# The first layer's attention taken by batch: four 32-row score tiles side by side, sums by a ones tile, division at the heads, mask addend on GpSimd

## The chip, the cores and the metric

The kernel runs on one core of a Trainium2 chip. Five engines work at once on their own instruction streams: TensorE (matrix products, weight loads beside them), VectorE, ScalarE, GpSimd and SyncE (which issues the transfers). They share the on-chip memory SBUF; TensorE writes into PSUM, eight banks of 128 partitions by 512 float32, and wait for one another on semaphores. The metric is the device time of one execution in microseconds (us), the median of several runs.

## The reference, cut to what matters

Four cross-attention layers run one after the other on x (16 batches of 128 tokens, 256 features) with a context of the same size. The change lies in the first, in float32:

```python
def attention(q, k, v, mask):            # 16 heads of 16 features
    scores = jnp.einsum('bhqd,bhkd->bhqk', q, k) / jnp.sqrt(jnp.float32(HD))
    scores = scores * mask - 10000.0 * (1.0 - mask)
    probs = jax.nn.softmax(scores, axis=-1)
    return jnp.einsum('bhqk,bhkd->bhqd', probs, v)
# layer 0: x += o(attention(ln1 x, ln1 x, mask 1)); x += co(attention(ln2 x, context, mask 2));
#          x += w2(gelu(w1(ln3 x)))      # 256 -> 1024 -> 256
```

Both masks are applied in full, whatever they hold.

## The kernel before

The function `layer0` (line 136) takes the batches in eight pairs (NB = 2). The attention of a pair is cut into units of four heads of one batch: a score tile of 128 queries by 4 x 128 keys fills one PSUM bank. There are U = 8 units of self attention and 8 of cross attention a pair, 4 units a batch.

All engines run the same eleven bodies of 16 steps (`bodies`, line 260): three written out, a loop over j = 3 to 7, three written out. In body g the cross units of pair g - 2 take steps 0 to 7 and the self units of pair g steps 8 to 15 (`unit`, line 268). Beside the units stands a table of linear parts (`BESIDE`, line 250), with the step and the offset of the pair: T0, T1, T2 are the transposes of the three layer norms, q, k, v and cq, ck, cv the projections, o and co the output projections, f0 to f3 the hidden parts and y0, y1 the outputs of the feed-forward. Bodies 0 and 1 have self attention alone, body 2 both attentions, bodies 3 to 7 everything, bodies 8 and 9 cross attention and feed-forward, body 10 feed-forward alone.

Each engine executes its stream in the order in which the code writes it out, so an instruction that waits holds back all behind it. A unit u goes this way:

- GpSimd, two steps ahead: `mask_keys` (line 393) copies the keys four times, each copy with all rows but those of one head set to zero (km). A product over 128 rows then gives four heads' scores at once.
- TensorE: `scores` (line 508), one product of 128 x 128 by 128 x 512. The profile shows a float32 product as two records.
- VectorE, `softmax_step` (line 737), all in step u: multiply by the mask out of PSUM into ring_e (line 748), then the reciprocal of the unit before (753), add the addend -10000 (1 - mask) (756), negated maxima (758).
- ScalarE, step u + 1: `exponentials` (614), four activations of 128 x 128, each with an accumulator for the sum of its rows.
- GpSimd, step u + 1: `norm` (406) multiplies the unit by the reciprocals (409).
- TensorE, step u + 3: `turn` (517), four transposes into the turn bank; ScalarE, step u + 4: `copy_turned` (622) into ring_t; TensorE, step u + 5: `times_v` (525), four products into column tiles of 32, at once with each other; ScalarE: `copy_heads` (627) after each second unit.

In a step TensorE does scores, linear part, `times_v`, `turn` (line 540); ScalarE exponentials, `copy_turned`, the affine or hidden part of the linear one, the tanh of the step before (`gate`), the heads (634); VectorE `softmax_step`, the reading of the linear part, the gate of the step before (`gated`), then at fixed steps statistics and normalisation of the layer norms (761). GpSimd takes the inverse deviations (`inverse_std`) and the biases of the residual (`add_bias`). The linear parts have four PSUM banks in three groups (line 216); scores have two, the turn bank and the heads' bank one each.

SyncE loads the pairs' inputs, context and masks one body ahead (line 349). After this layer a barrier follows, then the other three layers.

Of the kernel before, what the change touches and what calls it, by code (L numbers as in the profile page):

```python
# [14 lines left out]
ALU = mybir.AluOpType  # L15
# [3 lines left out]
P = 128  # L19
# [116 lines left out]
def layer0(nc, v):  # L136
# [8 lines left out]
    RE, RT, RK = 4, 2, 4  # L145

    L_E, L_T, L_P, L_V, LEAD_K = 1, 3, 4, 5, 2
    PAIR_ROWS = 2 * HD0
    with ExitStack() as ctx:  # L150
# [28 lines left out]
        qT = [sb(n, [P, 2, TOK]) for n in ("qT", "cqT")]  # L179
# [5 lines left out]
        km = sb("km", [P, RK, BANK])  # L185
        ring_e = sb("ring_e", [P, RE, BANK])
        ring_t = sb("ring_t", [P, RT, BANK])
# [3 lines left out]
        z_sum = sb("z_sum", [P, RE, QUAD])  # L191
        z_inv = sb("z_inv", [P, RE, QUAD])
# [11 lines left out]
        bq_scaled = sb("bq_scaled", [P, 4])  # L204

        def row(name):
            return rows[:, ROWS[name]:ROWS[name] + D]

        score_bank = [psum[:, j, :] for j in range(2)]
        turn_bank = psum[:, 2, :]  # L210
        pv_bank = psum[:, 3, :]

        entry = Banks(ctx, nc, "entry", ["T0", "q", "k", "v"], [psum[:, 4, :]])
        middle = Banks(ctx, nc, "middle", ["o", "T1", "ck", "cq", "cv"], [psum[:, 5, :]])
        post = Banks(ctx, nc, "post", ["co", "T2", "f0", "f1", "f2", "f3", "y0", "y1"],
                     [psum[:, 6 + j, :] for j in range(2)])
        for banks in (entry, middle, post):  # L220
            events += banks.full_ev + banks.out_ev
# [12 lines left out]
        (keys_masked, scores_done, scores_mul, scores_add, max_done, exp_done, z_inv_done, probs_done, turned,  # L234
         probsT_done, pv_done) = (event(n, STEPS, credit=2) for n in (
             "keys_masked", "scores_done", "scores_mul", "scores_add", "max_done", "exp_done", "z_inv_done",
             "probs_done", "turned", "probsT_done", "pv_done"))
        heads_out = event("heads_out", U, credit=2)
# [5 lines left out]
        dve_consts = sem("dve_consts")  # L244
        vm_zeroed = sem("vm_zeroed")
        ident_step = sem("ident_step")

        BESIDE = {0: [("T2", -3)], 1: [("f0", -3)], 2: [("T0", 0), ("f1", -3)], 3: [("q", 0)], 4: [("k", 0)],  # L250
                  5: [("f2", -3)], 6: [("o", -1)], 7: [("f3", -3)], 8: [("v", 0)], 9: [("y0", -3)],
                  10: [("T1", -1)], 11: [("y1", -3)], 12: [("ck", -1)], 13: [("co", -2)], 14: [("cq", -1)],
                  15: [("cv", -1)]}
        BODIES = R0 + 3

        LIKE = 5
# [1411 lines left out]
```

## Time and profile before

| | us |
|---|---|
| median of 3 runs | 1520.36 (1518.43 to 1522.3) |
| profiled execution | 1517.32 |
| its span, first to last instruction | 1515.6 |
| TensorE busy | 1330.7 (88%) |
| VectorE busy | 1003.3 (66%) |
| ScalarE busy | 888.4 (59%) |
| GpSimd busy | 649.5 (43%) |
| mean granted TensorE clock | 0.965 |

The rows write PE for TensorE, PEld for its weight loads, DVE for VectorE, ACT for ScalarE and POOL for GpSimd. Busy time is the union of an engine's instructions. A group of instructions is told by line, engine, operation and tiles written and read; behind the bar come the busy time, the mean of one in ns, and the idle time of its engine just before it with what ended that. TensorE's records overlap: the start of the next is a better measure of what a group costs than its own length.

### The profile page before, as it was taken

To read this page: it belongs to the slowest core of one execution; us is meant where nothing else is said; L and a number is where in the kernel's file an instruction comes from. 1 tells how busy PE (TensorE), PEld (TensorE's weight loads), DVE (VectorE), ACT (ScalarE), POOL (GpSimd) and SP (SyncE) were. 2 spreads that over 40 slices of the span, in tenths; PEclk is the share of its full clock that TensorE was granted. 3 is DMA by queue.
4 is the path that set the end of the run, shared out by engine and by line. 5 is a ranking of instruction groups with operands and counts; after the bars stand their busy time and mean duration, and the time that the engine had idled before them with its cause. 6 is when DMAs were issued, how large, how long until landed. Compare 5 with 4: busy or idle time off the path is not lost. (4 is left out here: it accounts for less than half of the span.)

```text
span 1515.6 us, 29849 instructions
## 1 busy us (share of the span) xinstructions
PE 1330.7 (88%) x9586; PEld 999.7 (66%) x9586; DVE 1003.3 (66%) x2031; ACT 888.4 (59%) x3038; POOL 649.5 (43%) x615
## 2 busy tenths in 40 slices
PE   4678898898989776589999999999999999996897
PEld 2444565565656454478888888888888888884464
DVE  3477777777777844376666666676676667664354
ACT  2476767677776734365656656555565555553443
POOL 3487676766666632023334333333333333342000
PEclk9899999999999998789999999999999999998899
DMA  4030000000000000010000000000000000000110
GB/s 158 1 140 18 5 15 3 14 10 7 10 7 3 11 0 1 28 43 2 8 1 9 0 0 7 0 7 0 0 7 0 7 0 0 2 1 1 51 42 28
DMA packets 18509, 24.54 MB, mean 16 GB/s; under 512 B 1360, under 2 KB 16912, under 8 KB 18064
## 3 DMA queue, kind: packets, MB, share of 16 engines
q1 hardware_dynamic: 18448, 23.77, 4.8%
q8 instruction: 33, 0.54, 0.2%
q14 instruction: 28, 0.23, 0.1%
HBM read 21.67 MB, written 2.10 MB: 16 GB/s over the span
## 5 line engine op out<-in xcount | busy, mean ns | idle before, releaser
L953 POOL TENSOR_TENSOR prob<-prob,l_z_inv 128x512 f32<-128x512 f32 x256 | 261.2, 1042 | 457.2 <-DVE l_z_inv L1194 457.2
L1113 ACT ACTIVATE prob<-psum,l_neg_max 128x256 f32<-128x256 f32 x512 | 236.0, 473 | 240.5 <-DVE l_neg_max L1188 240.5
L618 ACT ACTIVATE ring_e<-ring_e,neg_max 128x128 f32<-128x128 f32 x512 | 199.4, 395 | 98.8 <-DVE neg_max L758 98.3
L409 POOL TENSOR_TENSOR ring_e<-ring_e,z_inv 128x512 f32<-128x512 f32 x128 | 174.2, 1361 | 139.5 <-DVE z_inv L753 139.5
L1188 DVE TENSOR_REDUCE l_neg_max<-psum 128x2 f32<-128x512 f32 x256 | 163.9, 682 | 10.6 <-PE psum L1007 10.6
L1035 PE MATMUL psum<-pT,vs 128*64 128x256 f32 x1024 | 138.8, 391 | 6.7 <-DVE aTl L1204 6.7
L1019 PEld LDWEIGHTS psum<-ident,prob 128*128 128x128 f32 x1024 | 109.8, 141 | 49.0 <-issue 45.4
L1019 PE MATMUL psum<-ident,prob 128*128 128x128 f32 x1024 | 139.9, 280 | 0.0
L521 PE MATMUL psum<-ident,ring_e 128*128 128x128 f32 x512 | 85.7, 292 | 50.7 <-ACT ring_t L625 49.7
L1199 DVE COPY pT<-psum 128x512 f32<-128x512 f32 x128 | 88.1, 689 | 51.0 <-PE psum L1019 51.0
L521 PEld LDWEIGHTS psum<-ident,ring_e 128*128 128x128 f32 x512 | 55.8, 144 | 81.5 <-issue 77.3
L1113 ACT ACTIVATION_READ_ACCUMULATOR prob<-psum,l_neg_max 128x1 f32 x512 | 103.7, 203 | 0.0
L1204 DVE TENSOR_TENSOR aTl<-psum,aTh 128x256 fp32r<-128x256 f32 x128 | 54.4, 425 | 74.2 <-ACT aTh L1128 74.2
L618 ACT ACTIVATION_READ_ACCUMULATOR ring_e<-ring_e,neg_max 128x1 f32 x512 | 98.1, 192 | 0.0
L1035 PEld LDWEIGHTS psum<-pT,vs 128*64 128x64 f32 x1024 | 63.2, 136 | 43.0 <-issue 5.9
L758 DVE TENSOR_REDUCE neg_max<-ring_e 128x4 f32<-128x512 f32 x128 | 87.8, 686 | 4.4
L1007 PE MATMUL psum<-kh,qh 64*128 64x256 f32 x512 | 85.8, 331 | 4.2 <-ACT prob L1113 4.2
L625 ACT COPY ring_t<-psum 128x512 f32<-128x512 f32 x128 | 73.0, 570 | 19.7 <-PE psum L521 19.5
L989 PE MATMUL psum<-zuh,wzh 128*128 128x256 f32 x256 | 74.4, 291 | 11.2 <-DVE zul L1230 11.2
L471 PE MATMUL psum<-w,hid 128*128 128x256 f32 x256 | 65.5, 415 | 19.5 <-DVE hid L710 19.5
L399 POOL TENSOR_TENSOR km<-kT,head_rows 128x512 f32<-128x512 f32 x64 | 71.2, 1116 | 23.1 <-issue 13.9
L399 POOL TENSOR_TENSOR km<-ckT,head_rows 128x512 f32<-128x512 f32 x64 | 78.4, 1226 | 0.0
(196 smaller groups left out, 3510.3 us busy)
## 6 DMA issues: line engine op xcount, KB each, us to landing
wz_raw<-wz_in SPq DMA_DIRECT2D x2, 1536.0 KB, 10.4
x_in<-x SPq DMA_DIRECT2D x8, 256.0 KB, 2.7
cT<-ctxT SPq DMA_DIRECT2D x8, 256.0 KB, 2.7
w<-w_in SPq DMA_DIRECT2D x2, 1024.0 KB, 11.5
l_ub<-ctx_in SPq DMA_DIRECT2D x8, 256.0 KB, 2.8
cg<-ctx_in SPq DMA_DIRECT2D x4, 512.0 KB, 3.5
out<-fin SPq DMA_DIRECT2D x4, 512.0 KB, 2.8
wi_raw<-wi_in SPq DMA_DIRECT2D x1, 1536.0 KB, 15.2
```

Of the source, the lines that this page charges most:

```text
L399: pool.tensor_tensor(km[:, n % RK, :].rearrange("p (h k) -> p h k", h=QUAD), kT[a][:, half, b * P:(b + 1) * P].unsqueeze(1).broadcast_to([ ...
L409: pool.tensor_tensor(p, p, z_inv[:, n % RE, :].unsqueeze(2).broadcast_to([P, QUAD, P]), ALU.mult)\
L521: last = nc.tensor.transpose(turn_bank[:, h * P:(h + 1) * P], ring_e[:, n % RE, h * P:(h + 1) * P], ident[:, :])
L618: last = nc.scalar.activation(e, e, ACT.Exp, bias=neg_max[:, n % RE, h:h + 1], accum_out=z_sum[:, n % RE, h:h + 1])
L758: nc.vector.tensor_reduce(neg_max[:, n % RE, :], e, AX.X, ALU.max, negate=True)\
L953: pool.tensor_tensor(e, e, z_inv[:, t % RE, h, :].unsqueeze(2).broadcast_to([P, 2, D]), ALU.mult)\
L1007: last = mm(score_bank[h][:, qt * D:(qt + 1) * D], q[qp][rows, pair % 2, qt, b, :], k[kp][rows, pair % 2, :, b, :], start=(qp, kp) == (0, ...
L1019: last = nc.tensor.transpose(turn_bank[h][:, kt * D + qt * P:kt * D + (qt + 1) * P], prob[:, t % RE, h, qt * D + kt * P:qt * D + (kt + 1) ...
L1035: last = mm(pv_bank[h * HD1:(h + 1) * HD1, :], vs[:, pair // 2 % 2, b, kt, at:at + HD1], pT[:, h, kt * D:(kt + 1) * D], start=kt == 0, sto ...
L1113: last = nc.scalar.activation(prob[:, t % RE, h, qt * D:(qt + 1) * D], score_bank[h][:, qt * D:(qt + 1) * D], ACT.Exp, bias=neg_max[:, t % ...
L1188: nc.vector.tensor_reduce(neg_max[:, t % RE, h, :], score_bank[h].rearrange("p (t c) -> p t c", t=2), AX.X, ALU.max, negate=True).then_inc ...
L1199: nc.vector.tensor_copy(pT[:, 1, :], turn_bank[1]).then_inc(copied[1].sem, 1)
```

## The change

Lines of the change that the text speaks of; names as above.

- The queries, not the keys, are masked: `affine` for q and cq writes two copies of the transposed queries, one with the odd and one with the even heads' rows set to zero (scale and bias by `parity`), four activations in place of two. `mask_keys` and km go.
- `scores` runs once a batch, a step ahead of its first unit, at steps 3, 7, 11 and 15: 16 products with 32 rows of contraction, each on its own four rows-of-32 tile and, by tile, in its own PSUM bank (four score banks). Unit j of the batch is row tile j.
- VectorE multiplies the first two units of a batch in the first step and the other two in the second. GpSimd adds the addend (`add_mask`). The maxima follow on VectorE in the next step (L_M = 1), at its head.
- Exponentials have no accumulator, and nothing is multiplied between them and the transposes, which are in step u + 2, behind the linear part; `copy_turned` is in step u + 2 as well.
- `times_v` runs once a batch, at steps 2, 6, 10 and 14: 16 products as before, then 8 of 256 columns with a tile of ones as weights, which put the sum of each head's exponentials into the other half of the bank, on that head's rows.
- VectorE's `divide`, one step later (3, 7, 11, 15), takes the reciprocal of the sums (128 x 256, out of PSUM) and multiplies the heads by it into oT. `copy_heads` and the reciprocals of 128 x 4 go.
- The linear parts share two banks in turn. The table is written anew: cv at step 0 of the next body, f1 ahead of T0 in step 2, ck at 9, y0 at 11, co at 12, cq at 13, y1 at 15.
- Rings of eight instead of four for ring_e and of two for ring_t.

```diff
-    RE, RT, RK = 4, 2, 4
-    L_E, L_T, L_P, L_V, LEAD_K = 1, 3, 4, 5, 2
+    RE = 8
+    L_M, L_E, L_T, L_P, LEAD_S, L_V, L_N = 1, 1, 2, 2, 1, 6, 7
...
+        BESIDE = {0: [("T2", -3), ("cv", -2)], 1: [("f0", -3)], 2: [("f1", -3), ("T0", 0)], 3: [("q", 0)],
+                  4: [("k", 0)], 5: [("f2", -3)], 6: [("o", -1)], 7: [("f3", -3)], 8: [("v", 0)], 9: [("ck", -1)],
+                  10: [("T1", -1)], 11: [("y0", -3)], 12: [("co", -2)], 13: [("cq", -1)], 15: [("y1", -3)]}
...
+            def add_mask(a, i, u, ri, n):
+                e = ring_e[:, n % RE, :].rearrange("p (h k) -> p h k", h=QUAD)
+                add = (cross_add[:, u // QUAD, :] if a else self_add[:, :]).unsqueeze(1).broadcast_to([P, QUAD, P])
...
+                pool.wait_ge(*scores_mul.at(ri, n))
+                pool.tensor_tensor(e, e, add, ALU.add).then_inc(scores_add.sem, 1)
...
             def scores(a, i, u, ri, n):
...
+                for h in range(QUAD):
+                    half, t = divmod(h, 2)
+                    for j in range(QUAD):
+                        rows = slice(j * PAIR_ROWS, (j + 1) * PAIR_ROWS)
+                        last = nc.tensor.matmul(score_bank[j][:, h * P:(h + 1) * P],
+                                                qT[a][rows, t, half, b * P:(b + 1) * P],
+                                                kT[a][rows, half, b * P:(b + 1) * P], start=True, stop=True)
...
             def times_v(a, i, u, ri, n):
...
+                for half in range(2):
+                    for t in range(2):
+                        for j in range(QUAD):
+                            at, h = (2 * j + t) * PAIR_ROWS, 2 * half + t
+                            nc.tensor.matmul(pv_bank[j * PAIR_ROWS:(j + 1) * PAIR_ROWS, half * P:(half + 1) * P],
+                                             vm[a][:, b, half, at:at + PAIR_ROWS],
+                                             ring_t[:, (n + j) % RE, h * P:(h + 1) * P], start=t == 0, stop=t == 1)
+                for t in range(2):
+                    for j in range(QUAD):
+                        last = nc.tensor.matmul(pv_bank[j * PAIR_ROWS:(j + 1) * PAIR_ROWS, 2 * P:4 * P], ones[:, t, :],
+                                                ring_t[:, (n + j) % RE, :].rearrange(
+                                                    "p (c t q) -> p c t q", c=2, t=2)[:, :, t, :],
+                                                start=t == 0, stop=t == 1)
...
-                    last = nc.scalar.activation(e, e, ACT.Exp, bias=neg_max[:, n % RE, h:h + 1],
-                                                accum_out=z_sum[:, n % RE, h:h + 1])
+                    last = nc.scalar.activation(e, e, ACT.Exp, bias=neg_max[:, n % RE, h:h + 1])
...
+            def divide(a, i, u, ri, n):
...
+                dve.wait_ge(*pv_done.at(ri, n // QUAD))
+                nc.vector.reciprocal(z_inv[:, :], pv_bank[:, 2 * P:4 * P]).then_inc(z_inverted.sem, 1)
...
+                nc.vector.tensor_tensor(oT[a][:, :, b * P:(b + 1) * P],
+                                        pv_bank[:, 0:2 * P].rearrange("p (c q) -> p c q", c=2),
+                                        z_inv[:, :].rearrange("p (c q) -> p c q", c=2), ALU.mult)\
...
+                    if unit(j, g, s - L_M):
+                        maxima(*unit(j, g, s - L_M)[3:])
+                    for k in {0: (0, 1), 1: (1, 2)}.get(s % QUAD, ()):
+                        if unit(j, g, s + k):
+                            multiply(*unit(j, g, s + k))
+                    if (s - L_N) % QUAD == 0 and unit(j, g, s - L_N):
+                        divide(*unit(j, g, s - L_N))
```

## Rows read from the trace of the kernel before

**Rows 1.** The page: engines' busy time, and the exponentials among the costliest groups.
```profile
PE 1330.7 (88%) x9586; PEld 999.7 (66%) x9586; DVE 1003.3 (66%) x2031; ACT 888.4 (59%) x3038; POOL 649.5 (43%) x615
...
L618 ACT ACTIVATE ring_e<-ring_e,neg_max 128x128 f32<-128x128 f32 x512 | 199.4, 395 | 98.8 <-DVE neg_max L758 98.3
```
**Rows 2.** Windows: stretch, length, busy PE, PEld, DVE, ACT, POOL, clock, transfers.
```profile
24.66:68.78 44.12, 29.52 (x153) 17.42 (x153) 22.32 (x47) 20.62 (x82) 19.90 (x18) 0.85 0.02 7
68.78:96.31 27.53, 18.69 (x100) 10.36 (x98) 20.90 (x41) 16.78 (x72) 23.25 (x21) 1.00 0.07 18
96.31:152.30 55.99, 43.98 (x296) 26.46 (x288) 44.62 (x93) 41.58 (x170) 43.72 (x41) 1.00 0.26 98
152.30:221.60 69.30, 61.21 (x364) 40.74 (x364) 53.12 (x107) 49.28 (x186) 47.22 (x41) 0.95 0.04 11
...
290.00:358.40 68.40, 60.13 (x364) 39.84 (x364) 53.19 (x108) 49.29 (x186) 47.22 (x41) 0.98 0.03 10
...
498.10:557.00 58.90, 46.01 (x276) 31.17 (x276) 33.61 (x68) 31.44 (x110) 26.06 (x24) 0.94 0.01 3
557.00:639.30 82.30, 53.33 (x254) 38.02 (x254) 38.60 (x70) 38.26 (x122) 20.26 (x17) 0.85 0.00 1
```
**Rows 3.** Waits of the full body 290.0 to 358.4: us in total, times, longest.
```profile
PE psum L453 <- DVE ln L671: 5.4, 2, 3.8
```
**Rows 4.** Timeline of one unit in body 0: start, length, instruction, idle before.
```profile
36.47 0.18 DVE L753 RECIPROCAL z_inv<-z_sum 128x4 f32<-128x4 f32 x1 [1.12 <-ACT ring_e L618]
...
37.98 0.40 ACT L618 ACTIVATE ring_e<-ring_e,neg_max 128x128 f32<-128x128 f32 x1 [1.54 <-DVE neg_max L758]
...
39.53 0.56 ACT L625 COPY ring_t<-psum 128x512 f32<-128x512 f32 x1
39.66 0.18 DVE L753 RECIPROCAL z_inv<-z_sum 128x4 f32<-128x4 f32 x1 [1.12 <-ACT ring_e L618]
```
**Rows 5.** Timeline of TensorE over one step of a full body.
```profile
276.10 0.43 PE L535 MATMUL psum<-ring_t,cvm 128*32 128x128 f32 x8
276.45 0.66 PE L521 MATMUL psum<-ident,ring_e 128*128 128x128 f32 x4
276.95 1.02 PE L514 MATMUL psum<-km,qT 128*128 128x512 f32 x2
277.81 1.89 PE L471 MATMUL psum<-wco,coT 128*128 128x256 f32 x8
```
**Rows 6.** Timeline of TensorE in the second layer, two tiles side by side.
```profile
701.82 0.28 PE L1007 MATMUL psum<-kl,qh 64*128 64x256 f32 x2
701.94 0.29 PE L1007 MATMUL psum<-kh,ql 64*128 64x256 f32 x2
...
702.50 1.08 PE L1035 MATMUL psum<-pT,vs 128*64 128x256 f32 x8
```
**Rows 7.** Single lines over the span: shortest, median and longest in ns.
```profile
L753 DVE RECIPROCAL z_inv<-z_sum x128: 159/169/180, 29.5 to 589.3; 128x4 f32<-128x4 f32 x128
L1194 DVE RECIPROCAL l_z_inv<-l_z_sum x256: 144/156/169, 661.5 to 1381.3; 128x2 f32<-128x2 f32 x128
L399 POOL TENSOR_TENSOR km<-kT,head_rows x64: 1034/1040/1490, 22.4 to 484.9; 128x512 f32<-128x512 f32 x64
L671 DVE TENSOR_SCALAR ln<-x_in,mean_var,rstd x16: 400/412/1127, 8.5 to 436.4; 128x256 f32<-128x256 f32 x16
```
**Rows 8.** Timeline after the hidden part f0 of a full body.
```profile
295.21 0.84 ACT L584 ACTIVATE ring_g<-psum,cols 128x256 f32<-128x256 f32 x2
...
299.93 0.65 PE L453 MATMUL psum<-ident,ln 128*128 128x128 f32 x4 [3.76 <-DVE ln L671]
300.42 3.08 PE L462 MATMUL psum<-lnT,w 128*128 128x256 f32 x8
```
**Rows 9.** Groups of the full body 290.0 to 358.4 on VectorE and ScalarE.
```profile
L758 DVE TENSOR_REDUCE neg_max<-ring_e 128x4 f32<-128x512 f32 x16 | 11.0, 686 | 0.5
...
L592 ACT ACTIVATE ring_g<-ring_g 128x512 f32<-128x512 f32 x4 | 2.6, 646 | 0.0
```

More of the change, by code:

```diff
@@ new lines, in layer0, with lin @@
+        BODIES = R0 + 3
+        LIKE = 5
+        FILLED = [n for s in range(STEPS) for n in BESIDE.get(s, [])]
+        OFF = dict(FILLED)
+        PLACE = {name: (k % 2, k // 2) for k, (name, _) in enumerate(FILLED)}
+        lin_bank = [psum[:, 6 + j, :] for j in range(2)]
+        lin_full = [event(f"linear{j}_full", (len(FILLED) + 1 - j) // 2) for j in range(2)]
+        lin_out = [event(f"linear{j}_read_out", (len(FILLED) + 1 - j) // 2) for j in range(2)]
+        def lin(name):
+            return lin_bank[PLACE[name][0]]
@@ new lines, in free, with full, out, counts @@
+        def free(name, i):
+            bank, k = PLACE[name]
+            return lin_out[bank].at(i - OFF[name], k - 1)
+        def full(name, i):
+            bank, k = PLACE[name]
+            return lin_full[bank].at(i - OFF[name], k)
+        def out(name, i):
+            bank, k = PLACE[name]
+            return lin_out[bank].at(i - OFF[name], k)
+        def counts(name, g):
+            bank, k = PLACE[name]
+            order = [n for n, _ in FILLED if PLACE[n][0] == bank]
+            n, at = 1, (g, k)
+            while True:
+                at = (at[0], at[1] + 1) if at[1] + 1 < len(order) else (at[0] + 1, 0)
+                if at[0] >= BODIES or 0 <= at[0] + OFF[order[at[1]]] < R0:
+                    return n
+                n += 1
@@ L222, in layer0, with start @@
+        def start(bank):
+            order = [n for n, _ in FILLED if PLACE[n][0] == bank]
+            return len(order) + next(g * len(order) + k for g in range(BODIES) for k, n in enumerate(order)
+                                     if 0 <= g + OFF[n] < R0)
         input_in = event("input_in", 1, 16)
@@ L305, in _ @@
             for e in events:
-                sp.nop().then_inc(e.sem, e.credit * e.per)
+                if e not in lin_full and e not in lin_out:
+                    sp.nop().then_inc(e.sem, e.credit * e.per)
+            for bank in range(2):
+                sp.nop().then_inc(lin_full[bank].sem, start(bank))
+                sp.nop().then_inc(lin_out[bank].sem, start(bank))
             def load_x(i):
@@ L454, in norm_turn, with features_out @@
                                                    ln[k][:, b, c * P:(c + 1) * P], ident[:, :])
[L455 to L457 removed]
+                filled(name, last, g)
+            def features_out(i, name, w, at, src, g):
                 ps = bank(name, i)
@@ L463, in features_out, with tokens_out @@
                                                 src[:, c, :], start=c == 0, stop=c == 1)
-                full(name, last)
-            def tokens_out(i, name, w, at, src, chunks, batches):
+                filled(name, last, g)
+            def tokens_out(i, name, w, at, src, chunks, batches, g):
                 ps = bank(name, i)
@@ L541, in body @@
                 for s in range(STEPS):
-                    if unit(j, g, s):
-                        scores(*unit(j, g, s))
+                    if (s + LEAD_S) % QUAD == 0 and unit(j, g, s + LEAD_S):
+                        scores(*unit(j, g, s + LEAD_S))
                     for name, i in beside(j, g, s):
```

353 lines of the change are left out of this document (160 added, 193 removed).

## The prediction

> **What bounds the kernel now.** I read the page first: TensorE is busy for 88% of the span [rows 1], but that is a mean over three parts. Then the windows, cut at the first score multiplication of each self or cross sequence [rows 2]. The reader should see that the first layer ends at 639.3, so the change can only touch those 639 us. The stretches inside it differ. A full body, one turn of the loop with self attention, cross attention and feed-forward, takes 68.4 us with TensorE busy 60.1, VectorE 53.2, ScalarE 49.3, GpSimd 47.2 [rows 2]: TensorE sets it, with about 8 us of holes. The waits of that body name the largest hole: the transposes of the layer norms stand for VectorE's normalisation, 5.4 us in two places [rows 3]. The stretches with attention alone or without feed-forward (24.7 to 152.3) are different: TensorE is busy 29.5 of 44.1, 18.7 of 27.5 and 44.0 of 56.0 us [rows 2]. There a unit (four heads of one batch) takes 3.19 us, from one reciprocal on VectorE to the next [rows 4], although no engine works that long on it. It is a ring: the reciprocal waits for ScalarE's four exponentials (1.55 us from the first one's start to the copy behind them), and the mask addition and the maxima, which release the next exponentials, are queued behind the reciprocal. So two limits must be costed apart: TensorE's work in full bodies, the ring elsewhere.
>
> **The change, part by part.** The profiled execution took 1517.32 us around a span of 1515.6; the median of the runs is 1520.36, 3 us more. I cost against the former and add the 3 us at the end.
>
> *Scores.* Now 277.81 less 276.95, 0.86 us a unit, 3.44 us a batch of four units [rows 5]. After: 16 products of 32 rows, four side by side, each of 128 columns in two passes. A transpose has 128 columns as well: four take 276.95 less 276.45, 0.50 us, less what the first one pays about 0.11 each. Eight rounds give 0.9, with the change of tiling 1.05 us. Bounds: 0.9, and 32 × 0.11 = 3.5 us if nothing overlaps. I take 1.05, since tiles of 64 rows do run in pairs: two products of 256 columns start every 0.12 us [rows 6].
>
> *Values and sums.* Times-values costs 0.35 us a unit now (276.45 less 276.10), 1.4 a batch [rows 5]; as one piece of eight rounds about 1.0. The ones tile adds four rounds of 256 columns. The nearest row is the second layer's two column tiles: eight products in 1.08 us, 0.25 a round of two [rows 6]. That gives 0.95 if four run like two, 2.0 if only two do; I take 0.95, as the four-tile piece of rows 5 overlaps. A batch goes from 3.44 + 1.4 + 4 × 0.5 = 6.8 to 1.05 + 1.95 + 1.8 = 4.8 us of TensorE: 2.0 less, 64 us over 32 batches, if TensorE were the limit afterwards.
>
> *VectorE* loses the addition and the 0.17 us reciprocal [rows 7] of each unit, and gets one divide per batch: a 128x256 reciprocal out of PSUM and a 128x256 product. The narrow reciprocals show the price of a column: 169 ns for four columns, 156 for two [rows 7], 6.5 ns each, so 256 columns cost 0.15 + 1.66 = 1.8 us. Bounds: 0.41 (a 128x256 operation at its median [rows 7]) and 4.8 (longest four less shortest two, 18 ns a column). With the product 2.2 us a batch. VectorE then has some 45 us in a full body.
>
> *GpSimd* loses two operations a unit and gets one, the mask addition. The masking operation of the same shape takes 1.04 us at the median and 1.49 at most [rows 7]; I take 1.1. It has slack everywhere: 47 becomes about 24 us. What is queued behind its new wait for the multiplication is the two tiny operations for the inverse deviation, and VectorE's normalisation waits for them; the additions run ahead of that.
>
> *ScalarE* loses the accumulators and the copies of the heads, and gets two affines more per query projection (0.37 us each, from the 0.84 us of two [rows 8]). Four exponentials take 1.55 us [rows 4]; without the accumulator read each should start about 0.29 after the last, by the overlap of the pairs in rows 8, so 1.25 us. Bounds 1.25 and 1.55. The Trainium skill ("ScalarE: Activation LUTs", what ACT_TABLE_LOAD costs) has activations back to back overlap by about 93 ns; the trace agrees with it (two of 0.47 in 0.84), and by the page the four would take an estimated 1.27.
>
> *Order.* This is what speaks against the change. Maxima of a unit now come one step later on VectorE, at the head of the step in which ScalarE wants them; and the copy out of the turn bank is in the same step as its transposes, which stand behind TensorE's projection, and ahead of ScalarE's affine or hidden part for that projection. So each step with a feed-forward part is a round trip: maxima 0.69 [rows 9], exponentials 1.25, copy 0.45 (0.56 [rows 4] less overlap), four hidden activations 1.5 [rows 8], polynomial and product 1.15 (two passes of at most 0.69 [rows 9]); the step after it maxima, exponentials, copy, tanh 0.65 [rows 9], gate 0.65. The two linear banks instead of four are covered, except where a projection waits for the one two before it.
>
> I laid one full body out in these durations, from the end of times-values in step 14:
> - scores 1.05, y1 3.6, its output and the normalisation (0.42 + 0.74): T2 at 6.05, cv, turn, copy, affine: f0 at 10.2 to 12.0;
> - turn, copy, hidden, polynomial, normalisation: 16.5, T0. Against now, the wait that f1 is put ahead of shrinks from 3.76 [rows 8] to about 2.4;
> - steps 2 to 8, the round trips: VectorE through its gate of f0 at 22.6, of f1 at 27.8, polynomial of f2 35.4, gate 39.1, polynomial of f3 44.3, gate and normalisation 48.7;
> - T1 and the turn behind it wait for exponentials: 51.2; values 1.95, scores 1.05, y0 3.6, turn, co: 60.05; addition and statistics 1.75; maxima, exponentials, turn, values: 66.3.
> So 66.3 us, of which TensorE works 51. The saved TensorE work (8 us) mostly becomes holes. There is also the clock: after the hole of 3.76 us a projection took 3.08 instead of 1.9 us [rows 8]; mean granted clock 0.98 means one such stretch at 1.2 GHz per body. In my layout TensorE has 3 us of work between 40 and 51, so a second one is likely, 1.7 us. I take 68.0 against a mean of 69.2 for the five (498.1 less 152.3, over 5): 6 us gained in all.
>
> Attention alone: per batch VectorE needs 4 × 1.2 (maxima and multiplication, 0.69 each [rows 9] and 0.6 from start to start) + 2.2 plus half a microsecond of waiting for the first addition, ScalarE 4 × 1.7 and a stretch behind the divide: 8.2 us a batch, 2.05 a unit, not 3.19. Twice a batch in body 0, 9 us; starting 1 us earlier (scores need no masked keys); the way from the last maxima through values, divide and o to the next self sequence 13.7 instead of 17 us; the second self sequence with T1, ck, cq about 19.7 instead of 27.5 us. Together 22; less 2 for half-rate stretches, 20. Body 2 (96.3 to 152.3, 56.0 us) laid out likewise gives 44.6, less 1.4 for the clock: 10 gained. Body 8 (498.1 to 557.0) has no self units: the chain through f3, gate and T1 is as long as before, 60 against 58.9; in bodies 9 and 10 (82.3 us) y1 now stands ahead of T2's normalisation: 2 lost. Sum: 20 + 10 + 6 - 3 = 33. 1517.3 - 33 = 1484; with the 3 us of the median **1487 us**.
>
> **Rivals.**
> *TensorE stays the limit and the round trips hide* (f parts finish earlier than I laid them): full bodies at 62, six us below mine, 1487 - 30 = 1457. For it: all four engines lose work. Against it: ScalarE already waits 98 us for maxima in this layer, with the maxima a step earlier [rows 1].
> *The round trip costs more and eats most of the gain*: with the contended durations VectorE shows beside GpSimd (normalisation up to 1.13 us a piece [rows 7]) my first layout gave 73.2: 5 × 5.2 = 26, 1513.
> *It turns the sign*: the same place, step 1 to step 8, but exponentials keep their 1.55 us: 0.3 us on 11 of the 16 steps, 3 to 4 us a body on top, 77; and 10 us in the first bodies: 1487 + 45 + 10 = 1542. It decides from 74.6 us a full body up (33/5 above mine).
> *The tiles don't run at once*, the change doesn't do what it says: 2.5 us a batch more, of which some 70% lie in the path: 32 × 2.5 × 0.7 = 56, 1543. Against it rows 5 and 6.
>
> **How the numbers follow.** Forecast (1470 to 1504) 0.55; TensorE stays the limit 0.15; most of the gain eaten 0.12; sign turned 0.12; tiles in turn 0.06. Range 1456 to 1516: it takes in the second and third case. A measurement of this kernel tells 0.3%, 4.6 us, from no change: faster is below 1515.8. Of the third case three quarters are faster, a part of the rest falls within: faster 0.78, same 0.06, slower 0.16.
>
> **What would show it.** The first layer should end near 606 (639 now), full bodies at 66 to 70 us with TensorE busy near 52 to 55 of them and its waits on ScalarE and VectorE up; scores near 1.05 and values with sums near 1.95 us a batch; reciprocal 1.8 to 2.3 us; four exponentials in 1.25; the mask addition 1.04 on GpSimd; two clock dips a body; body 2 about 46. Full bodies above 74 us, or a score batch of 3 us, would make the prediction wrong; bodies near 62 would make it too timid.

## The result

The kernel after takes 1536.44 us in the median (1527.40 to 1539.91), before 1520.36: the ratio is 1.0094, interval 1.0057 to 1.0132: slower, by less than 2%. The forecast was 1487 us. The profiled execution took 1539.91 us around a span of 1536.9. From the page of after (busy time; the granted clock in fortieths of the span; the queue that fetches TensorE's instructions):

```profile
PE 1308.2 (85%) x10866; PEld 1042.4 (68%) x10866; DVE 943.9 (61%) x1843; ACT 846.2 (55%) x2494; POOL 491.9 (32%) x490
...
PEclk8889898989888987889999999999999999998899
...
q8 instruction: 82, 1.34, 0.4%
```

Every engine is busy for less time than in [rows 1] (only the weight loads beside TensorE for more), and the kernel is slower. Windows of after, cut as in [rows 2]:

```profile
20.50:56.20 35.70, 25.35 (x234) 18.37 (x232) 18.46 (x35) 17.84 (x48) 12.07 (x11) 0.76 0.06 18
...
77.60:133.10 55.50, 41.72 (x455) 32.30 (x454) 38.20 (x70) 34.86 (x96) 25.46 (x24) 0.85 0.26 99
133.10:207.00 73.90, 57.60 (x527) 45.09 (x526) 46.49 (x84) 44.07 (x118) 26.95 (x25) 0.88 0.03 10
...
282.10:357.20 75.10, 58.81 (x527) 45.93 (x526) 46.51 (x84) 44.20 (x118) 26.93 (x25) 0.86 0.03 9
507.40:566.30 58.90, 43.13 (x358) 33.62 (x356) 29.67 (x57) 29.03 (x76) 14.37 (x14) 0.86 0.03 8
566.30:648.50 82.20, 51.66 (x312) 40.06 (x312) 34.05 (x60) 34.26 (x86) 13.41 (x12) 0.83 0.00 1
```

The balance, before less after:

| stretch | before | after | forecast | measured |
|---|---|---|---|---|
| start to first cross unit | 96.3 | 77.6 | -20 | -18.7 |
| body 2 | 56.0 | 55.5 | -10 | -0.5 |
| bodies 3 to 7 | 345.8 | 374.3 | -6 | +28.5 |
| body 8 | 58.9 | 58.9 | +1 | 0 |
| bodies 9, 10 | 82.3 | 82.2 | +2 | -0.1 |
| all behind the first layer | 876.3 | 888.4 | 0 | +12.1 |

So three things are to be explained: the full bodies (74.9 us in the mean against 69.2; four of the five take 75.1), body 2, and 12 us where no line was changed. The granted clock is 0.86 in a full body (0.98 in [rows 2]). The waits of the full body 282.1 to 357.2 (us in total, times, longest):

```profile
ACT ring_e L674 <- DVE neg_max L795: 18.3, 12, 3.6
ACT ring_t L681 <- PE psum L568: 12.6, 6, 6.2
DVE ring_g L747 <- ACT ring_g L639: 9.9, 4, 3.7
...
PE psum L492 <- DVE ln L717: 7.2, 3, 3.4
...
PE psum L568 <- ACT ring_t L681: 6.6, 4, 1.9
```

Every engine waits for the next one: a round trip, with TensorE's wait for the normalisation at 7.2 us where [rows 3] had 5.4. TensorE behind its holes (timeline of after: start, length, instruction, idle before):

```profile
275.51 1.17 PE L558 MATMUL psum<-ckT,cqT 32*128 32x128 f32 x32
...
293.74 1.11 PE L492 MATMUL psum<-ident,ln 128*128 128x128 f32 x4 [3.39 <-DVE ln L717]
294.64 1.06 PE L568 MATMUL psum<-ident,ring_e 128*128 128x128 f32 x4
295.63 1.94 PE L584 MATMUL psum<-ring_t,vm 128*32 128x128 f32 x32
297.34 1.93 PE L589 MATMUL psum<-ring_t,ones 128*32 128x256 f32 x16
299.20 1.42 PE L558 MATMUL psum<-ckT,cqT 32*128 32x128 f32 x32
...
309.85 3.66 PE L510 MATMUL psum<-wao,oT 128*128 128x256 f32 x8
...
313.90 1.08 PE L584 MATMUL psum<-ring_t,cvm 128*32 128x128 f32 x32
314.79 1.05 PE L589 MATMUL psum<-ring_t,ones 128*32 128x256 f32 x16
315.77 1.17 PE L558 MATMUL psum<-kT,qT 32*128 32x128 f32 x32
316.87 1.99 PE L501 MATMUL psum<-lnT,w 128*128 128x256 f32 x8
...
329.07 1.11 PE L492 MATMUL psum<-ident,ln 128*128 128x128 f32 x4 [2.89 <-DVE ln L717]
...
332.48 1.93 PE L584 MATMUL psum<-ring_t,cvm 128*32 128x128 f32 x32
334.19 1.93 PE L589 MATMUL psum<-ring_t,ones 128*32 128x256 f32 x16
336.05 1.75 PE L558 MATMUL psum<-kT,qT 32*128 32x128 f32 x32
337.73 3.72 PE L510 MATMUL psum<-w,hid 128*128 128x256 f32 x16
...
341.73 1.89 PE L510 MATMUL psum<-wco,coT 128*128 128x256 f32 x8
343.46 0.60 PE L568 MATMUL psum<-ident,ring_e 128*128 128x128 f32 x4
...
350.60 1.17 PE L558 MATMUL psum<-ckT,cqT 32*128 32x128 f32 x32
```

At 313.90 the batch of values, sums and scores costs 0.89 + 0.98 + 1.10 = 2.97 us, as priced (1.95 + 1.05). At 295.63 and 332.48 values and sums take 1.71 and 1.86 us from start to start, twice as long: the lower of the two clock levels (1.2 GHz against 2.4), both times behind a hole of some 3 us. There is a third such stretch, the projection of wao at 309.85. A granted clock of 0.86 over 75.1 us is, by estimate, 21 us at the lower level; 0.98 over the 68.4 us of before is under 3.

### The profile page after: what moved, and what is told of

It reads as the page before. It is cut to its first block and busy times, and to the rows that moved or that the text cites. A ratio compares the mean times of both kernels' runs of the same rounds, so it can differ in the third digit from the quotient of the medians.

```text
span 1536.9 us, 31339 instructions
## 1 busy us (share of the span) xinstructions
PE 1308.2 (85%) x10866; PEld 1042.4 (68%) x10866; DVE 943.9 (61%) x1843; ACT 846.2 (55%) x2494; POOL 491.9 (32%) x490
## 3 DMA queue, kind: packets, MB, share of 16 engines
q8 instruction: 82, 1.34, 0.4%
## 5 line engine op out<-in xcount | busy, mean ns | idle before, releaser
L674 ACT ACTIVATE ring_e<-ring_e,neg_max 128x128 f32<-128x128 f32 x512 | 163.8, 394 | 142.9 <-DVE neg_max L795 142.9
L568 PE MATMUL psum<-ident,ring_e 128*128 128x128 f32 x512 | 89.7, 304 | 79.7 <-ACT ring_t L681 75.7
L568 PEld LDWEIGHTS psum<-ident,ring_e 128*128 128x128 f32 x512 | 68.3, 157 | 103.1 <-ACT ring_e L674 91.3
L450 POOL TENSOR_TENSOR ring_e<-ring_e,cross_add 128x512 f32<-128x512 f32 x64 | 81.5, 1287 | 169.7 <-DVE ring_e L790 169.7
L450 POOL TENSOR_TENSOR ring_e<-ring_e,self_add 128x512 f32<-128x512 f32 x64 | 80.9, 1281 | 113.6 <-DVE ring_e L790 113.0
L1268 DVE TENSOR_TENSOR aTl<-psum,aTh 128x256 fp32r<-128x256 f32 x128 | 54.3, 424 | 71.9 <-ACT aTh L1192 71.9
L1071 PE MATMUL psum<-kh,qh 64*128 64x256 f32 x512 | 85.9, 331 | 12.3 <-issue 9.3
L802 DVE RECIPROCAL z_inv<-psum 128x256 f32<-128x256 f32 x32 | 56.1, 1754 | 59.8 <-PE psum L589 59.8
L501 PE MATMUL psum<-lnT,w 128*128 128x256 f32 x256 | 66.5, 407 | 16.4 <-ACT lnT L628 11.4
L1186 ACT COPY pT<-psum 128x512 f32<-128x512 f32 x128 | 76.4, 597 | 2.5 <-PE psum L1083 2.5
## 6 DMA issues: line engine op xcount, KB each, us to landing
w<-w_in SPq DMA_DIRECT2D x2, 1024.0 KB, 11.5
```

Source lines behind the costliest of these rows:

```text
L450: pool.tensor_tensor(e, e, add, ALU.add).then_inc(scores_add.sem, 1)
L568: last = nc.tensor.transpose(turn_bank[:, h * P:(h + 1) * P], ring_e[:, n % RE, h * P:(h + 1) * P], ident[:, :])
L674: last = nc.scalar.activation(e, e, ACT.Exp, bias=neg_max[:, n % RE, h:h + 1])
L1071: last = mm(score_bank[h][:, qt * D:(qt + 1) * D], q[qp][rows, pair % 2, qt, b, :], k[kp][rows, pair % 2, :, b, :], start=(qp, kp) == (0, ...
L1186: nc.scalar.copy(pT[:, 0, :], turn_bank[0]).then_inc(copied[0].sem, 1)
```

## The experiments

Times are medians; ratios are against the kernel before on the same chip. "Body" is the mean of bodies 3 to 7, from the first cross multiplication on VectorE of body 3 to that of body 8, over 5; the clock is the mean granted one over these five.

| run | us | ratio, interval | body | clock |
|---|---|---|---|---|
| pad_after | 1519.8 | 1.0027, 1.0008 to 1.0047 | 74.9 | 0.87 |
| pad_before | 1535.4 | 1.0111, 1.0078 to 1.0143 | 69.2 | 0.96 |
| fill_after | 1507.9 | 0.9944, 0.9921 to 0.9966 | 71.9 | 0.98 |
| lag_after | 1503.8 | 0.9914, 0.9889 to 0.9940 | 71.9 | 0.91 |
| addend_vector | 1508.3 | 0.9939, 0.9922 to 0.9955 | 71.6 | 0.92 |
| fill_addend | 1501.8 | 0.9904, 0.9889 to 0.9920 | 70.2 | 0.97 |
| copy_late | 1508.8 | 0.9946, 0.9929 to 0.9962 | 71.9 | 0.91 |
| copy_late_fill | 1496.6 | 0.9868, 0.9851 to 0.9884 | 69.8 | 0.97 |
| co_later | 1459.4 | 0.9621, 0.9601 to 0.9640 | 64.9 | 0.99 |
| co_later_alone | 1521.5 | 1.0025, 1.0013 to 1.0036 | 74.8 | 0.89 |
| co_later_no_fill | 1482.6 | 0.9768, 0.9740 to 0.9796 | 68.4 | 0.93 |
| addend_no_fill | 1480.4 | 0.9759, 0.9744 to 0.9775 | 68.5 | 0.91 |
| all_parts | 1460.7 | 0.9634, 0.9611 to 0.9656 | 64.8 | 0.98 |
| fewer_fills | 1458.9 | 0.9614, 0.9599 to 0.9628 | 64.1 | 0.98 |
| fill_before | 1546.0 | 1.0186, 1.0165 to 1.0207 | 71.1 | 0.98 |

**The 12 us outside the first layer.** Both kernels got instructions ahead of everything on TensorE, waits that are met already (two such lines make one instruction):

```diff
+            for _ in range(154):        # pad_after; 256 in pad_before
+                pe.wait_ge(consts_made, 1)
             pe.wait_ge(consts_made, 1)
             bodies(pe, body)
```

> The kernel after, with 77 more instructions (waits that are already met) on TensorE at its very start, nothing else. Reason for it: outside the first layer the kernel after is 12.1 us longer than before, though its code there is the same, and the packets of 16 KB with which TensorE's instructions are fetched go on through the rounds of the second layer (83 packets in all against 33), nine a round, where before has none. In the traces some 256 weight loads and products pass between two such packets. Counted so, the second layer's loop is 1,964 instructions, 7.67 packets; it starts 0.15 of a packet past a packet's edge before (it touches 8 packets) and 0.86 past one after (it touches 9). With 77 instructions more it starts at 0.16 again. Theory (the loop must touch no more than 8 packets): no fetching in the rounds, some 33 to 39 packets in all, a round of the second layer 91.2 us instead of 93.5, the whole 1524 us, 12 less than after; the first layer unchanged at 75.1 us a body. Rival (the fetching hangs on something else than where the loop starts, or it costs nothing and the 12 us are of the data): packets stay near 83, or the time stays at 1536.

> The kernel before, with 128 more instructions (waits already met) on TensorE at its start. The second layer's loop then starts 0.65 past a packet's edge and touches 9 packets. Theory: some nine packets a round are fetched as in after, a round takes 93.5 instead of 91.2 us, the whole 1532 us, 12 more than before. Rival (nothing hangs on where the loop starts): 1520 us and 33 packets.

The page's row of the fetches (that of after stands above), and the single line of one instruction that each round of the second layer has once (shortest, median, longest in ns; first and last start in us). Of after:

```profile
L1211 ACT CAST zuh<-l_ub x8: 614/657/657, 655.0 to 1303.6; 128x512 fp32r<-128x512 f32 x8
```

Of pad_after, page and line:

```profile
q8 instruction: 38, 0.62, 0.2%
```
```profile
L1212 ACT CAST zuh<-l_ub x8: 616/657/658, 655.7 to 1292.8; 128x512 fp32r<-128x512 f32 x8
```

Of pad_before:

```profile
q8 instruction: 78, 1.28, 0.4%
```
```profile
L1148 ACT CAST zuh<-l_ub x8: 614/657/657, 653.7 to 1301.6; 128x512 fp32r<-128x512 f32 x8
```

Seven rounds take 648.6 us in after, 637.1 in pad_after, 647.9 in pad_before; 637.0 in before, whose page has 33 packets. That is settled in both directions: 11.5 us hang on where the unchanged loop of the second layer starts. It is not spread over all rounds: the loop is passed six times, and in the trace of after each of the five passes behind the first has 9 fetches and takes 92.9 to 94.2 us, in pad_after none and 91.3. The count in the expectation was one packet too high: all four traces show 1,708 records of TensorE in a pass (1,556 products and weight loads, the rest waits and branches), 6.7 packets of 256 and not 7.67. So the loop touches 7 packets where it stays and 8 where it is fetched anew; the starting positions and what followed from them held.

The ratio of pad_after, 1.0027, tells best what the change does by itself. The pad itself takes some time: TensorE's first product starts at 10.2 us in pad_after (9.1 in after), at 15.5 in pad_before (9.4 in before) and at 18.3 in fill_before, whose pad is 154 instructions. That is why pad_before loses some 8 us more than the fetches explain: its first multiplication on VectorE starts 4.4 us later than before's (29.1 against 24.7), its body 8 ends 6.8 us later. All runs below have a pad where they need it for their loop to stay; they show 38 fetches each, fill_before 34.

**The clock.**

```diff
                 name = f"T{k}"
-                pe.wait_ge(*ln_done[k].at(i))
                 ps = bank(name, i)
+                for _ in range((3, 3, 1)[k]):
+                    nc.tensor.matmul(ps, ident[:, :], ident[:, :].unsqueeze(1).broadcast_to([P, QUAD, P]),
+                                     start=True, stop=True)
+                pe.wait_ge(*ln_done[k].at(i))
```

> The kernel after, with products that nobody reads (fp32, 128x512, the identity) ahead of TensorE's waits for the three normalised inputs: three ahead of T0 and of T1, one ahead of T2, into the linear bank that the transposes then overwrite. They fill holes of 3.4, 2.9 and 0.9 us and leave every wait as it is. By the count of instructions the second layer's loop starts 0.27 past a packet's edge and touches 8 packets, so 12 us should be gone for that reason alone (base 1524). Theory (the half-rate clock behind the holes costs about 6 us of the chain of a full body): granted clock 0.86 becomes 0.95 or more in full bodies, these take 69 to 71 us instead of 75.1, the whole 1495 to 1502. Rival (the chain is the round trip of the four engines, and TensorE at half rate hides in its own holes): bodies stay at 74 to 77, the whole 1522 to 1534.

```profile
194.20:265.20 71.00, 59.16 (x539) 44.49 (x538) 46.54 (x83) 43.91 (x118) 26.99 (x25) 0.98 0.03 9
265.20:337.80 72.60, 59.50 (x539) 44.30 (x538) 46.53 (x83) 43.91 (x118) 26.96 (x25) 0.98 0.03 9
```

These windows of two full bodies show 0.98 where after has 0.86. A body is 3.0 us shorter and body 2 takes 48.9 us instead of 55.5. The whole is 12 us under pad_after, although TensorE was given 6.3 us of useless work a body: the theory holds, its size was put too high (69 to 71 expected; 71.9 measured, 1507.9 against 1495 to 1502). With the products ScalarE's wait for the maxima is 18.3 us as before them, so the round trip was left as it was and the body is shorter all the same. The cross-check is the same edit on the kernel before:

> The kernel before with the same unread products ahead of its three normalised inputs (and 154 instructions of padding, so that the second layer's loop starts at 0.15 of a packet as before). Its granted clock in full bodies is 0.98, one short stretch at half rate a body. Theory (the half-rate clock is what the change brought in, before had little of it): 1512 to 1522, within 0.4% of before. Rival (one stretch behind a hole of 3.8 us costs 1.7 us of each chain as well): 1504 to 1511. Other rival (TensorE sets before's pace and the products add to it): 1525 or more.

Its second rival came true: bodies of 71.1 against 69.2, TensorE busy 66.27 of 71.40 us (60.13 of 68.40 in [rows 2]), 28 us slower. Of these some 9 are the pad at its start and 9.5 the five bodies; the rest, some 10, lies in the other bodies, which have the products too. Here, where TensorE is the limit and its clock is granted, the products only cost.

**The order.**

```diff
-    L_M, L_E, L_T, L_P, LEAD_S, L_V, L_N = 1, 1, 2, 2, 1, 6, 7
+    L_M, L_E, L_T, L_P, LEAD_S, L_V, L_N = 1, 2, 3, 3, 1, 7, 8
```

> The kernel after with a longer lag in the first layer's attention: exponentials two steps behind the scores' multiplication instead of one, turn and copy three instead of two, values 7 instead of 6, divide 8 instead of 7 (and 77 instructions of padding, so that the second layer's loop starts at 0.16 of a packet; base 1524). The maxima of a unit are then made a step before ScalarE wants them, as in before. Theory (the round trip maxima, exponentials, copy, affine or hidden part, polynomial, maxima is what sets a full body): ScalarE's wait for the maxima, 18.3 us of a body, falls below 8, bodies 68 to 71 us instead of 75.1, the whole 1494 to 1506. Rival (the half-rate clock sets it): bodies 73 to 76, the whole 1518 to 1530. Against both: the divide of units 4 to 7 of cross attention moves into the step of its projection co, which then waits for it, up to 2 us a body.

In the waits of a full body of lag_after (274.3 to 346.0):

```profile
ACT ring_t L682 <- PE psum L568: 24.9, 12, 4.9
...
ACT ring_e L675 <- DVE neg_max L796: 2.6, 1, 2.6
PE psum L510 <- DVE coT L807: 2.4, 1, 2.4
```

ScalarE's wait for the maxima falls from 18.3 to 2.6 us, as the theory said, but its wait for the turn doubles and the body gives only 3.0 us. The next two runs go after what took its place: L_P = 4 (copy_late), and this with the unread products (copy_late_fill).

> The run with the longer lag (lag_after: 1503.8 us, full bodies of 71.7 us), and ScalarE's copy out of the turn bank one step later still, four steps behind instead of three. In lag_after ScalarE stands 24.9 us of a body in that copy, waiting for a turn that TensorE makes behind the projection of the step, with the hidden part or affine of an earlier projection queued behind the copy. Theory (the copy is the second half of the round trip): this wait falls below 8 us, full bodies 67 to 69.5 us, the whole 1482 to 1492. Rival (the waits of the copy are slack, and the transposes of the layer norms set the body through VectorE): bodies 71 to 72, the whole 1499 to 1506.

> copy_late with the unread products of fill_after ahead of the waits for the normalised inputs (three, three, one). Theory (order and clock are two causes that add): granted clock above 0.95 in full bodies, these 2 to 3.5 us shorter than in copy_late, 64.5 to 67 us, the whole 1470 to 1482. Rival (with the round trip gone the holes are short and the products now take time themselves, 6.3 us a body of TensorE at full clock): bodies the same as in copy_late or up to 3 us longer, the whole 1485 to 1505.

copy_late is a miss: the wait for the turn falls to 13.4 us, the body stays at 71.9 and the whole is 5 us longer (by the ratios, whose intervals overlap, no clear loss). The copy was slack, as its rival said. TensorE's own wait for the normalisation is 7.4 us of that body, as it was in after (7.2); that this sets the body is not shown. The products give 2.1 us a body and 12 in all: within the step of 2 to 3.5 us that was expected, but from a longer body, so that 1496.6 is far above the 1470 to 1482. Then the wait for coT:

```diff
-                  12: [("co", -2)], 13: [("cq", -1)], 15: [("y1", -3)]}
+                  12: [("cq", -1)], 13: [("co", -2)], 15: [("y1", -3)]}
...
-                    if s == 13 and i2 is not None:
+                    if s == 14 and i2 is not None:
                         inverse_std(i2, 2)
```

> copy_late_fill with the projections co and cq changed over (cq in step 12, co in step 13; the inverse deviation behind it in step 14), since with the longer lag the divide that co reads is in step 12: in lag_after co waited 2.4 us a body for it. Theory: that wait goes, bodies 1 to 2 us shorter than in copy_late_fill, 5 to 12 us of the whole. Rival (co's addition and statistics feed the normalisation for T2 in step 15, which becomes late in turn): no change, or up to 5 us more.

> The kernel after with nothing but co and cq changed over, as in co_later, at the lags of after (77 instructions of padding; to be compared with pad_after, 1519.8 us, bodies of 75.1, body 8 of 59). In co_later the change-over took 37 us off copy_late_fill, three times what the wait of co for the divide explains; 4.4 us a full body and 13 in the bodies after the last full one. Theory (what it gives is the earlier query of the next cross attention, whose scores stand before y1: that holds at any lag): 1485 to 1500, bodies 70 to 72. Rival (the gain came from the wait for the divide, which the lags of after do not have): 1515 to 1525, bodies 74.5 to 76.

> co_later without the unread products (77 instructions of padding instead). It says what the clock is worth once the order is mended. Theory (the clock costs what it cost between copy_late and copy_late_fill, 2.4 us a body and 12 of the whole): 1468 to 1476, bodies 66.5 to 68.5, granted clock 0.93. Rival (with short holes the clock stays up by itself): 1456 to 1464, bodies near 65 at a clock of 0.97. Rival (order and clock bind each other): above 1480.

```profile
260.20:324.40 64.20, 57.40 (x546) 43.39 (x538) 47.29 (x83) 43.49 (x118) 27.45 (x25) 1.00 0.03 10
```

The window is a full body of co_later: 64.2 us at full clock. The change-over gives 4.9 us a body and 37 us in all on top of copy_late_fill (24 in the five bodies, 3.4 in body 2, 7.1 in body 8), and nothing on top of after (1521.5 against 1519.8): the rival was right there, it pays only where the longer lag has put the divide in front of co. That it pays twice the 2.4 us of the wait I can't derive from rows; what I expected of the earlier query is refuted by co_later_alone. Without the products the same kernel is at 1482.6, 23 us slower and 3.5 us a body: theory and first rival (1468 to 1476, 1456 to 1464) had less, and the second rival, that order and clock bind each other (above 1480), came true. What the products give hangs on the order: 3.0 us a body on top of after, 2.1 at the longer lag, 3.5 with the change-over as well.

**The addend on GpSimd.** The lines go into VectorE's body, with the same addition behind its wait for the multiplication, and out of GpSimd's.

```diff
                    for k in {0: (0, 1), 1: (1, 2)}.get(s % QUAD, ()):
                        if unit(j, g, s + k):
                            multiply(*unit(j, g, s + k))
+                    if unit(j, g, s):
+                        add_mask(*unit(j, g, s))
```

> The kernel after with the mask addend back on VectorE, one addition of 128x512 per unit behind the multiplication of its step, GpSimd left with deviations and biases (77 instructions of padding: to be compared with pad_after, 1519.8 us, full bodies of 75.1). Theory (moving the addend was right; what VectorE's 1.38 us gate, 1.49 us polynomial and 1.67 us normalisation lose beside GpSimd is 2.5 us a body and less than the 16 additions of 0.6 us cost on VectorE): bodies 76 to 80 us, the whole 1524 to 1545. Rival (GpSimd's 1.27 us per unit and what it slows on VectorE is a main cause of the slow body): bodies 70 to 73, the whole 1495 to 1510.

The rival was right: 11.5 us less than pad_after. But the granted clock rose as well, from 0.87 to 0.92, so that not all of it is GpSimd's; with the products in both, the move gives 1.7 us a body (fill_after 71.9, fill_addend 70.2). Groups on VectorE over a full body, first of after (282.1 to 357.2), then of addend_vector (276.1 to 347.9): count, busy us, mean ns, idle before.

```profile
L756 DVE SCALAR_TENSOR_TENSOR hid<-ring_g,ring_h 128x512 f32<-128x512 f32 x4 | 3.5, 863 | 4.6 <-ACT ring_g L647 4.6
L747 DVE TENSOR_SCALAR ring_g<-ring_g 128x512 f32<-128x512 f32 x4 | 2.8, 692 | 9.9 <-ACT ring_g L639 9.9
L717 DVE TENSOR_SCALAR ln<-x,mean_var,rstd 128x256 f32<-128x256 f32 x4 | 2.4, 640 | 0.0
```
```profile
L794 DVE TENSOR_TENSOR ring_e<-ring_e,cross_add 128x512 f32<-128x512 f32 x8 | 5.9, 742 | 0.0
...
L753 DVE SCALAR_TENSOR_TENSOR hid<-ring_g,ring_h 128x512 f32<-128x512 f32 x4 | 2.8, 690 | 1.8 <-ACT ring_g L644 1.8
L744 DVE TENSOR_SCALAR ring_g<-ring_g 128x512 f32<-128x512 f32 x4 | 1.7, 428 | 7.0 <-ACT ring_g L636 7.0
L714 DVE TENSOR_SCALAR ln<-x,mean_var,rstd 128x256 f32<-128x256 f32 x4 | 1.5, 405 | 0.0
```

VectorE takes on 16 additions of 0.74 us a body, 54.3 us busy instead of 46.5, and the body is 3.3 us shorter. An addition takes 1.29 us on GpSimd, and beside it the gate, the polynomial's first half and the normalisation lose 170 to 260 ns a piece. Does this add to the clock, and does it hold at the longer lag?

> The kernel after, at its own lags and order, with the unread products of fill_after and the addend on VectorE of addend_vector: the clock and GpSimd's share taken out, the order left as the prediction laid it out. Theory (the layout of 66.3 us and 1.7 for the clock was right, and what was missed are clock and contention, which add): 75.1 less 3.6 less 3.5, 67.5 to 69 us a body, the whole 1488 to 1500. Rival (they overlap, because the round trip of the four engines is longer than laid out): bodies 70 to 71.5, the whole 1502 to 1510.

> co_later_no_fill (1482.6 us, bodies of 68.3, clock 0.93) with the addend on VectorE. In all_parts the same move gave nothing (64.9 before and after), with TensorE busy 59.1 of 64.9 us, 6.3 of it unread products. Theory (TensorE had become the limit there; without the products GpSimd's share is in the chain again): bodies 64.5 to 66.5, the whole 1460 to 1472. Rival (at the longer lag GpSimd is hidden): bodies 68 to 69.5, the whole 1480 to 1490.

> co_later (1459.4 us, full bodies of 64.9) with the mask addend on VectorE, as in addend_vector, where it took 11.5 us off the whole and 3.4 us off a body. Theory (GpSimd's 1.27 us per unit and what VectorE loses beside it lie in the chain here too): bodies 62 to 63.5 us, the whole 1440 to 1452. Rival (VectorE, 47 us busy of a body in co_later, becomes 55 and now sets the pace, or TensorE with 57 to 58 us does): bodies 64.5 to 67, the whole 1457 to 1475.

> all_parts (1460.7 us, bodies of 64.9) with fewer unread products: two ahead of T0 and of T1, none ahead of T2, 3.6 us a body instead of 6.3. Theory (TensorE is the limit of all_parts and the products are part of it; the clock stays up with fewer): bodies 62.5 to 64, the whole 1444 to 1456. Rival (the clock falls again behind the holes that open): bodies 65 to 67, the whole 1460 to 1475.

fill_addend: 70.2 us a body and 1501.8, the rival. Together the two give 4.7 us, not 3.0 + 3.3. At the longer lag the move gives nothing, with products or without (64.8 against 64.9, 68.5 against 68.4): the rival of addend_no_fill was right, the lag hides GpSimd. What I had taken all_parts for, TensorE at its limit because of the products, falls with it; fewer_fills confirms that, as taking away 2.7 us of them moved the body by 0.7 and the whole not measurably. fewer_fills has the lowest time, 1458.9 us, 3.9% under before and by the ratios 4.8% under after and 4.1% under pad_after; co_later and all_parts can't be told from it, their intervals overlap.

## Why the prediction was wrong

It was 49 us too low in the medians. By the balance of the profiled executions it is 54: 34.5 in the full bodies, 9.5 in body 2, 12.1 behind the first layer, and 2 the other way. The steps that failed are, in order: the clock's term of 1.7 us, GpSimd's "slack everywhere", the end of the layout, and nothing put down for the other layers.

*Most prices were right.* Batch of scores 1.10 (1.05), values and sums 1.87 (1.95), four exponentials 1.28 (1.25), the reciprocal at 1.75 (1.8). Four affines take 1.94 us where the prediction's 0.84 and twice 0.37 give 1.58. From the timeline and the single lines of after:

```profile
303.50 1.94 ACT L628 ACTIVATE qT<-psum,bq_scaled,parity 128x256 f32<-128x256 f32 x4
...
307.31 1.28 ACT L674 ACTIVATE ring_e<-ring_e,neg_max 128x128 f32<-128x128 f32 x4 [1.35 <-DVE neg_max L795]
```
```profile
L802 DVE RECIPROCAL z_inv<-psum x32: 1747/1757/1758, 37.5 to 607.6; 128x256 f32<-128x256 f32 x32
```

The reciprocal never varies by more than 11 ns. The Trainium skill's repeat count of 8 ("VectorE: DVE Perf Modes", the walkthrough of the 8-slice pipeline) had made it an estimated 2.3; the measurement decides, and the sum would not have moved. The attention-only start is right in its sum (-18.7 for -20), in part by luck: its four terms add up to 21.1 and not to the 22 written, the first multiplication starts 4.2 us earlier (24.7 to 20.5) where 1 was laid out, and the stretch behind it gives 8.4 (44.1 to 35.7) where 12.3 were.

*The clock: "a second one is likely, 1.7 us".* This term of the sum was mis-sized. The prediction had itself taken 8 us of work off TensorE and turned them into holes, and then carried the clock of before over with one dip added. After runs at 0.86, with three stretches at the lower level a body and not two; values and sums stand in two of them and take twice their time, on the chain. From T0 to the scores pass 5.46 us in after (293.74 to 299.20) and 2.84 in fill_addend (below); from the values behind T1 to y0 5.25, laid out at 1.95 + 1.05. The unread products got back 3.0 us a body net of their own cost, 3.5 at a better order, and 6.6 of the 9.5 us that body 2 missed; with the addend on VectorE they gave only 1.4 a body (71.6 to 70.2) and 0.9 in body 2 (52.7 to 51.8). So the clock's share is not a fixed sum, and body 2 stays open in part.

*GpSimd: "It has slack everywhere".* The duration was close (1.29 for 1.1), the reading wrong: the engine had slack, the chain not. Multiplication, addition, maxima, exponentials stand in a row, and the step behind waits for them; what GpSimd slows on VectorE stands there as well. It is 3.3 us a body alone, and 1.7 with the clock held up by the products. The numbers for this were at hand: with contended durations [rows 7] the first layout gave 73.2 us, and it was made a rival at 0.12 instead of the forecast.

*The layout.* Its milestones, counted from the start of the scores in step 15 (after: 275.51; fill_addend, where clock and GpSimd are taken out: 268.04):

| | laid out | after | fill_addend |
|---|---|---|---|
| T0 starts | 16.5 | 18.2 | 18.5 |
| turn behind T1 ended | 51.2 | 57.0 | 53.0 |
| co ended | 60.05 | 68.0 | 61.7 |
| next scores | 66.3 | 75.1 | 69.5 |

TensorE's timeline in fill_addend:

```profile
268.04 1.59 PE L557 MATMUL psum<-ckT,cqT 32*128 32x128 f32 x32
...
286.58 0.60 PE L491 MATMUL psum<-ident,ln 128*128 128x128 f32 x4
...
289.42 1.17 PE L557 MATMUL psum<-ckT,cqT 32*128 32x128 f32 x32
...
321.05 1.08 PE L583 MATMUL psum<-ring_t,cvm 128*32 128x128 f32 x32
...
329.75 0.60 PE L567 MATMUL psum<-ident,ring_e 128*128 128x128 f32 x4
...
337.50 1.17 PE L557 MATMUL psum<-ckT,cqT 32*128 32x128 f32 x32
```

With the two causes out the round trip runs as laid out to within 2.0 us up to co; part of that is the products themselves, which end 0.9 us after the normalisation for T0 and more than that after the one for T1. The last piece was laid out at 6.25 us and takes 7.1 in after, 7.8 in fill_addend, where VectorE has the additions too: ScalarE's copy of the turn before (0.56) stands between the exponentials and the last turn, and was left out there. So of the 6.9 us by which a body (74.9) exceeds the 68.0 of the sum, 3.0 are clock and GpSimd, which took 4.7 together where 1.7 were put down, and 3.9 are the layout: 70.2 us in fill_addend for 66.3, with the products' own delay and what its clock of 0.97 costs in it. The order did cost, where the prediction had feared it ("what speaks against the change"), and the longer lag shows it: ScalarE's wait for the maxima was real, 18.3 us, and taking it away gave 3.0 us a body, at a clock of 0.91 for 0.87.

*The rivals.* "Turns the sign" gave the right side by the wrong mechanism: exponentials did not keep 1.55 us. Its deciding point, 74.6 us a full body, was just passed (74.9), and the padded kernel stands at +0.3%. "Costs more", 73.2 us by contended durations, was the nearest in mechanism. "TensorE stays the limit" and "tiles in turn" are refuted by the rows.

*What was not considered* is 12 us of instruction fetching in another layer.

Open is how co's wait, the lag and the clock bind each other: the change-over gave 0 at the lag of after, 3.5 us a body at the long lag without the products (71.9 to 68.4) and 4.9 with them.

## What to carry to other kernels

Work taken off the engine that sets the pace is a gain only as far as the order can use it; if it becomes holes, the clock can fall too, as here from 0.98 to 0.86, and both belong in the sum. When a step is handed to an idle engine, ask what stands behind it in the chain, not how idle the engine is. And when a change alters the length of code ahead of a long loop, compare the rounds of that loop and the count of instruction packets before anything else is explained.

## What the hardware showed beside that

- A loop on TensorE of 1,708 records (6.7 packets) is kept when it starts so that it touches 7 packets of 16 KB, and fetched anew in each pass, nine packets, when it touches 8: 33 to 38 packets in all against 78 to 82, 91.3 us a pass against 92.7 to 94.8 in the two kernels with fetches. The Trainium skill ("Runtime: NRT & Kernel Launch", "Instruction fetch mechanics") gives TensorE room for 2048 instructions in blocks of 256, which agrees with the 16 KB of a packet and with about 256 records between two of them (1.34 MB in 82 packets). A loop of 8 blocks would fit that room, and here it was not kept; that one block goes to the fetch ahead, as nine packets for eight touched suggest, is not shown. The page calls the fetch mostly hidden, and here some 2.3 us a pass are not. A second queue had 48 packets in after and in pad_after (28 in before), and nothing in the times follows it.
- Products that nobody reads, 6.3 us a body ahead of waits, took 23 us off co_later and added about 19 us to the kernel before, the pad taken off.
